# Decoder layer on one core: both row normalisations of the cross attention move from VectorE to ScalarE, and a GpSimd subtraction gets a later place

## The reference, cut to what matters

```python
def _layernorm(x, axis=-1, eps=1e-05):
    m = jnp.mean(x, axis=axis, keepdims=True)
    v = jnp.var(x, axis=axis, keepdims=True)
    return (x - m) / jnp.sqrt(v + eps)

def _L0_xattn_ref(input1, input2, theta_w, theta_b, phi_w, phi_b, g_w, g_b, ln_gamma, ln_beta, out_w, out_b):
    theta_x = jnp.einsum('ld,bdt->btl', theta_w, input2) + theta_b
    phi_x = jnp.einsum('ld,bdt->blt', phi_w, input1) + phi_b[:, None]
    p = jax.nn.softmax(jnp.einsum('btl,bls->bts', theta_x, phi_x), axis=-1)
    g_x = jnp.einsum('ld,bdt->btl', g_w, input1) + g_b
    t_x = jnp.einsum('bts,bsl->blt', p, g_x)
    mu = jnp.mean(t_x, axis=(1, 2), keepdims=True)
    var = jnp.var(t_x, axis=(1, 2), keepdims=True)
    h = jax.nn.relu((t_x - mu) * jax.lax.rsqrt(var + LN_EPS) * ln_gamma + ln_beta)
    return jnp.einsum('ol,blt->bot', out_w, h) + out_b[None, :, None] + input2

x = x + _L0_attn_ref(_layernorm(x, axis=-1), ...)
x = x + _L0_xattn_ref(_layernorm(x, axis=-1), ctx_2048, ...)
x = x + _L0_ffn_ref(_layernorm(x, axis=-1), ...)
```

## Time and profile before

| what | value |
|---|---|
| time, median of 3 runs | 3100.88 us (3097.79 to 3101.97) |
| the profiled execution's own time | 3099.93 us |
| its span, first to last instruction | 3098.2 us |
| PE busy in the span | 2804.7 us (91%) |
| DVE, ACT, POOL busy | 1327.8, 887.2, 846.1 us |
| cross attention in the span | from about 722.8 to 1134.2 us |

### The profile page before, as it was taken

How to read it: one execution, slowest core, us unless ns; L and a number is a source line. 1 busy time by engine, 2 the same in 40 slices (tenths; PEclk the granted TensorE clock), 3 DMA queues, 4 the chain that set the end, 5 groups by cost and what they waited for, 6 DMA issues and landing times.

```text
span 3098.2 us, 46522 instructions
## 1 busy us (share of the span) xinstructions
PE 2804.7 (91%) x16538; PEld 2355.9 (76%) x16538; DVE 1327.8 (43%) x2273; ACT 887.2 (29%) x1637; POOL 846.1 (27%) x1123
## 2 busy tenths in 40 slices
PE   6989999997787740799999999999999999999998
PEld 6855555476676630699999999999999999999997
DVE  6756777577888862113213213223223223223111
ACT  1126666623444422112112112112112112112110
POOL 4546777512222317201111110110210210210110
PEclk9999999998988965799999999999999999999999
DMA  3102222341212114203203213212112212122110
GB/s 103 41 2 39 46 46 46 60 112 46 81 42 80 61 39 106 66 20 105 79 25 109 73 45 95 66 58 88 60 59 85 64 65 86 55 72 82 37 48 20
DMA packets 97119, 194.60 MB, mean 63 GB/s; under 512 B 22126, under 2 KB 23822, under 8 KB 96848
## 3 DMA queue, kind: packets, MB, share of 16 engines
q1 hardware_dynamic: 75168, 131.85, 14.8%
q0 software_dynamic: 21808, 60.65, 6.3%
HBM read 148.77 MB, written 38.94 MB: 61 GB/s over the span
## 4 chain that ended last, share of the span: by engine, by line
PE 59%; issue 2%; DMA 1%; DVE 0%; POOL 0%; ACT 0%; SPq 0%; DVEq 0%; POOLq 0%
PE ex_hid L1709 29%; PE ex_acc L102 9%; PE ex_acc L103 9%; PE ex_acc L104 9%; PE ex_xb L1679 1%; DMA ex_raw<-in_w_tiles_dram 1%; DVE ex_w_l L1611 0%; ACT ex_w_h L1580 0%; DVE ex_w_l L1614 0%; DMA ex_ys<-xn_dram,ex_rows_in 0%; POOL out_dram L1561 0%; SPq L1507 0%; DMA ex_ys<-slot_table_dram 0%; ACT ex_w_h L1582 0%; DVE ex_ys L1622 0%
## 5 line engine op out<-in xcount | busy, mean ns | idle before, releaser
L1630 DVE SCALAR_TENSOR_TENSOR ex_h0l<-ex_hid,ex_h0h 128x640 fp32r<-128x640 f32 x128 | 105.6, 825 | 690.5 <-ACT ex_h0h L1589 683.2
L1630 DVE SCALAR_TENSOR_TENSOR ex_h1l<-ex_hid,ex_h1h 128x640 fp32r<-128x640 f32 x128 | 105.6, 825 | 613.8 <-ACT ex_h1h L1589 562.6
L1589 ACT ACTIVATE ex_h0h<-ex_hid 128x640 fp32r<-128x640 f32 x128 | 90.3, 706 | 739.0 <-PE ex_hid L1709 726.5
L1589 ACT ACTIVATE ex_h1h<-ex_hid 128x640 fp32r<-128x640 f32 x128 | 90.3, 706 | 737.7 <-PE ex_hid L1709 705.4
L652 DVE TENSOR_REDUCE at_nb<-at_ring 128x2 f32<-128x512 f32 (+1 forms) x384 | 246.9, 686 | 121.7 <-PE at_ring L758 121.7
L1525 POOL COPY ex_gi<-ex_slot_gather 128x1 int32 (+1 forms) x84 | 16.4, 196 | 904.9 <-PE ex_xb L1679 896.7
L102 PE MATMUL ex_acc<-ex_w_h,ex_h1h 128*128 128x512 f32 x640 | 254.8, 398 | 0.0
L102 PE MATMUL ex_acc<-ex_w_h,ex_h0h 128*128 128x512 f32 x640 | 253.4, 396 | 0.0
L103 PE MATMUL ex_acc<-ex_w_l,ex_h0h 128*128 128x512 f32 x640 | 250.3, 391 | 0.0
L103 PE MATMUL ex_acc<-ex_w_l,ex_h1h 128*128 128x512 f32 x640 | 250.2, 391 | 0.0
L104 PE MATMUL ex_acc<-ex_w_h,ex_h1l 128*128 128x512 f32 x640 | 249.8, 390 | 0.0
(11 more groups left out here) (271 smaller groups left out, 5980.0 us busy)
## 6 DMA issues: line engine op xcount, KB each, us to landing
ex_raw<-in_w_tiles_dram SPq DMA_DIRECT2D x256, 256.0 KB
x_in<-in_x_dram SPq DMA_DIRECT2D x32, 256.0 KB
act<-at_raw SPq DMA_DIRECT2D x128, 64.0 KB
at_recb<-o_rec_dram SPq DMA_DIRECT2D x16, 512.0 KB
k<-in_x_dram SPq DMA_DIRECT2D x32, 256.0 KB, 2.7
cx_ctx<-in_ctx_dram SPq DMA_DIRECT2D x16, 512.0 KB
out_dram<-cx_res SPq DMA_DIRECT2D x16, 512.0 KB
xn_dram<-cx_prob SPq DMA_DIRECT2D x16, 512.0 KB
```

The source lines that it names most:

```text
L1589: act.activation(h[f % 2][0][:], hid[:, :, 0:HB], ACT.Relu).then_inc(sm["h_hi"], 1)
L1630: dve.scalar_tensor_tensor(h[f % 2][1][:], hid[:, :, 0:HB], 0.0, f32(h[f % 2][0][:]), ALU.max, ALU.subtract).then_inc(sm["h_lo"], 1)
```

## The change

`norm_input` goes from DVE to ACT: (x - m)·r is done as r·x + (-m·r), an ACTIVATE of the Identity function with a scale and a bias per row. It stands at the head of ACT's tail, and in `front(0)` ACT does `norm_input` and `xin_hi` of each chain ahead of `ctx_hi`. The shift -m·r is made by POOL in the stage before, with two more small instructions a round. The second normalisation goes from DVE to ACT in the same form, behind `latent_hi` of theta and ahead of the splits of its own transposes; POOL makes its shift with two more small instructions a chain. And POOL's context remainder, in the tail, waits until both chains' `h_lo` are there.

```diff
@@ stage_attention, gpsimd, output projection
                 pool.tensor_tensor(t["rstd1"][:, bass.ds(CH * j, CH), 0], now, t["half"][:].to_broadcast([P, CH]),
                                    ALU.pow).then_inc(op["rstd_ready"], 1)
+                less = t["shift1"][:, bass.ds(CH * j, CH), 0]
+                pool.tensor_tensor(less, t["mv1"][:, bass.ds(CH * j, CH), 0], t["minus"][:].to_broadcast([P, CH]),
+                                   ALU.mult).then_inc(op["rstd_ready"], 1)
+                wait_apart(pool, op["rstd_ready"], 2 * j + 2, op["passed_pool"])
+                pool.tensor_tensor(less, less,
+                                   t["rstd1"][:, bass.ds(CH * j, CH), 0], ALU.mult).then_inc(op["shift_ready"], 1)
@@ stage_cross, gpsimd, tail
                 if ahead:
+                    wait_apart(pool, sm["h_lo"], CB * j + CB, sm["passed_pool"])
                     front(j + 1)
                 for c in chains:
                     n = CB * j + c
                     pool.wait_ge(sm["moments"], ONE + TPB * (n + 1))
                     pool.tensor_tensor(ve[:, c, :], mv[:, c, :, 1], t["eps"][:].to_broadcast([P, TPB]),
                                        ALU.add).then_inc(sm["eps"], 1)
+                    pool.tensor_scalar(less[:, c, :], mv[:, c, :, 0], -1.0, None, ALU.mult).then_inc(sm["rstd"], 1)
                     pool.wait_ge(sm["eps"], ONE + n + 1)
                     pool.tensor_tensor(rstd[:, c, :], ve[:, c, :], t["half"][:].to_broadcast([P, TPB]),
                                        ALU.pow).then_inc(sm["rstd"], 1)
+                    pool.wait_ge(sm["rstd"], ONE + 2 * n + 2)
+                    pool.tensor_tensor(shift[:, c, :], less[:, c, :], rstd[:, c, :], ALU.mult).then_inc(sm["shift"], 1)
@@ stage_cross, scalar
+            def norm_input(j, c):
+                n = CB * j + c
+                wait(act, sm["xin_lo"], n + 1 - CB)
+                for u in range(TPB):
+                    act.activation(xin[c][:, u, :], t["act"][:, TPB * n + u, :], ACT.Identity,
+                                   bias=t["shift1"][:, TPB * n + u, :], scale=t["rstd1"][:, TPB * n + u, :])\
+                        .then_inc(sm["xin"], 1)
             def front(j):
+                for c in chains:
+                    norm_input(j, c)
+                    xin_hi(j, c)
                 ctx_hi(j)
-                for c in chains:
-                    xin_hi(j, c)
             def tail(j, ahead):
+                if ahead:
+                    for c in chains:
+                        norm_input(j + 1, c)
...
                     latent_hi(j + 1, "theta")
                 for c in chains:
                     n = CB * j + c
+                    act.wait_ge(sm["shift"], ONE + n + 1)
+                    for u in range(TPB):
+                        act.activation(prob[c][:, u, :], res[c][:, u, :], ACT.Identity, bias=shift[:, c, u:u + 1],
+                                       scale=rstd[:, c, u:u + 1]).then_inc(sm["xn3"], 1)
+                for c in chains:
+                    n = CB * j + c
@@ stage_cross, vector
-            def norm_input(j, c):
-                n = CB * j + c
-                for u in range(TPB):
-                    dve.tensor_scalar(xin[c][:, u, :], t["act"][:, TPB * n + u, :],
-                                      t["mv1"][:, TPB * n + u, 0:1], t["rstd1"][:, TPB * n + u, :],
-                                      ALU.subtract, ALU.mult).then_inc(sm["xin"], 1)
             def front(j):
                 for c in chains:
-                    norm_input(j, c)
-                for c in chains:
                     xin_lo(j, c)
             def tail(j, ahead):
-                if ahead:
-                    for c in chains:
-                        norm_input(j + 1, c)
...
-                for c in chains:
-                    n = CB * j + c
-                    dve.wait_ge(sm["rstd"], ONE + n + 1)
-                    for u in range(TPB):
-                        dve.tensor_scalar(prob[c][:, u, :], res[c][:, u, :], mv[:, c, u, 0:1], rstd[:, c, u:u + 1],
-                                          ALU.subtract, ALU.mult).then_inc(sm["xn3"], 1)
```

More of the change, by code:

```diff
@@ L151, in _ @@
             pool.memset(t["half"][:], -0.5)
+            pool.memset(t["minus"][:], -1.0)
             pool.memset(t["eps"][:], EPS)
@@ L407, in stage_attention @@
         op = {n: s.sem("op_" + n) for n in ("wo_loaded", "wo_hi", "wo_lo", "hi", "lo", "y_ready", "x1_done", "stats",
-                                            "moments", "eps", "kept", "rstd_ready", "passed_pool", "passed_dve")}
+                                            "moments", "eps", "kept", "rstd_ready", "shift_ready", "passed_pool", "passed_dve")}
         x_loaded = [s.sem(f"op_x_loaded{c}") for c in range(CH)]
@@ L869, in stage_cross @@
         rstd = s.sb("cx_rstd", [P, CB, TPB])
+        less = s.sb("cx_less", [P, CB, TPB])
+        shift = s.sb("cx_shift", [P, CB, TPB])
         nmx = s.sb("cx_nmx", [P, CB, NTT])
@@ L886, in stage_cross @@
                  "gmv", "gsq", "gvar", "gve", "grstd", "centred", "scaled", "h_hi", "h_lo", "out", "x2", "stats",
-                 "moments", "eps", "rstd", "xn3", "x3T", "x3_hi", "x3_lo", "lgT", "lgT_kept", "logits",
+                 "moments", "eps", "rstd", "shift", "xn3", "x3T", "x3_hi", "x3_lo", "lgT", "lgT_kept", "logits",
                  "logits_kept", "passed_dve", "passed_pe", "passed_pool")
@@ L1734, in decoder_layer @@
         t["half"] = s.sb("half", [P, 1])
+        t["minus"] = s.sb("minus", [P, 1])
         t["eps"] = s.sb("eps", [P, 1])
@@ L1743, in decoder_layer @@
             t["rstd1"] = a.sb("rstd1", [P, NT, 1])
+            t["shift1"] = a.sb("shift1", [P, NT, 1])
             for n in ("theta_b", "phi_b", "g_b"):
```

## The result

| | before | after |
|---|---|---|
| median | 3097.77 us (3094.28 to 3101.97, 6 runs) | 3086.63 us (3084.44 to 3088.36, 6 runs) |
| ratio after / before | | 0.9962, 95% interval 0.9949 to 0.9975 |
| profiled execution, its span | 3099.93, 3098.2 us | 3084.44, 3082.7 us |

The change takes 11.1 us off by the medians; forecast were 3089.0 us and 11.9 off. The cross attention runs from 720.40 to the last copy of logits at 1122.31, 401.9 us, where it ran from 722.84 to 1134.05, 411.2 us. So the stage gives 9.3 of the 15.5 us by which the two spans differ. The rest isn't the change's: 2.4 lie ahead of the stage, though the change adds 0.5 there, and 3.8 behind it, where the code is the same. Such stages come out a few us apart from one execution to the next.

What follows compares the result with a forecast made beforehand. The cross attention's pass was taken as bound by a chain hopping between engines, none full. Seven passes 8.4, front 4.3, last tail -0.8 gave 11.9 us off, hence 3089.0 us; range 3079 to 3097.

Steps and rivals of the forecast that it cites:

- the likeliest case: The change works as summed, whole kernel at 3085 to 3094 us; chance 55%.
- POOL's new work: Output projection, ahead of the stage's barrier: two small POOL instructions and a wait add 0.65 us.
- The ACT normalisation: One normalisation on ACT with per-row scale and bias takes 0.81 us, each 0.71 when neighbours overlap.
- The head of the tail: `norm_input` on ACT delays the copy of `tx` by 0.62 us and PE's `phi` by 0.4 a pass.
- POOL's wait: Tail: DVE's scaled pair takes 1.4 us instead of 3.53, and the residual sum starts 1.1 us earlier.
- The second normalisation: Moved to ACT, with POOL's shift taking 1.44 us; the router starts at 886.85 instead of 888.09, 1.2 us a pass.
- clock, good: Rival: passes with a low PE clock turn to full clock, giving 3084 us; chance 6%.
- clock, bad: Rival: the four passes with good PE clock turn bad, costing 6 us, giving 3095; chance 15%.
- The front: Stage's start: ACT takes `xin` before the context, PE starts 4.3 us earlier; net 4.3, bounds 3.7 to 5.
- The last tail: With no front in it, from L962 to the router takes 6.4 us instead of 5.36; loss 0.8.
- The slower rival: POOL's moved remainder holds the residual sum L1165; each pass loses 1.7 us, 8.5 slower, 3109; chance 6%.

Runs made afterwards that it cites:

- the fourth experiment: The changed kernel with the first normalisation of the loop's tails back on DVE: 3078.22 us, ratio 0.9939 to the kernel before.
- the filled after: The changed kernel with matmuls that nothing reads in three idle gaps of PE per pass: 3070.69 us, ratio 0.9911 to the kernel before.
- the last experiment: The changed kernel with POOL's context remainder waiting for the residual sums instead of `h_lo`: 3132.02 us, ratio 1.0105 to the kernel before.
- the best version: The kernel before with POOL's wait, `xin` split before the context, and theta's remainder moved behind the router's splits, without filling matmuls: 3074.26 us, ratio 0.9928.
- the filled before: The kernel before with matmuls that nothing reads in three idle gaps of PE per pass: 3095.45 us, ratio 0.9994 to the kernel before.

## Why the prediction was right, and which step failed

**Sum.** 11.9 us off was forecast and 11.1 measured; 3086.63 lies within 3085 to 3094, the own range of the likeliest case. But the profiled stage gained 9.3, and 8.8 with the 0.5 that POOL's new work costs ahead of it, where the terms promised 11.9; and within the passes the parts differ more than the sum. That the median came so near is partly luck.

**The ACT normalisation: right.** Estimated at 0.81, one each 0.71. Measured: medians of 0.817 and 0.807 over 32 each, four in a row in 2.93 (850.64 to 853.57). The head of the tail loses 0.55 a pass (the fourth experiment), forecast was 0.4. With this move undone the median falls by 8.4, far more than the forecast gave it.

**POOL's wait: right as a mechanism, and its gain at the residual sum is the step that failed.** (1.1 us earlier in the forecast, behind the 0.4 lost at the tail's head; 1.5 counted from the centring.) The pair went to 1.41 and PE's idle 1.11 us went. But "the residual sum L1165 starts at 876.05 instead of 877.17" took PE's `phi` and `g` at full speed for granted, as in the pass that was read. "The other passes repeat it" was wrong: in before every second pass has the slow `phi`, and there the residual sum comes at 9.46, at 9.37 in the others, because the hold and the slow `phi` lie side by side. After has `phi` at the low clock in all seven passes, `g` is late, and the gain is hidden: 9.46, with the wait and without it. At full clock the step is there in full (7.87 against 9.37).

**The second normalisation: right.** From the start of POOL's `ve` to the end of the shift it took 1.32 (873.95 to 875.27), forecast 1.44. PE's transposes started 6.60 after the residual sum, forecast 6.7, and the router 10.70, forecast 10.8; before it was 10.92. Most of the 1.2 us forecast here was to come from the residual sum's being earlier; without that, 0.23 is left.

**What paid instead.** 0.85 a pass come from the router's matmuls: they are slow in no pass, where in before they are in every second. That is the rival "clock, good" in one place and "clock, bad" in another. The forecast gave both a chance, but as alternatives that moved the whole sum, and not as two halves that nearly cancel. The 0.85 has nothing to do with the reasons that the forecast gave, and that it made up for over half of the missing 1.5 is luck.

**The front: right.** PE's first `phi` matmul was forecast 4.3 us earlier, with POOL's new work ahead of the barrier counted in. Timelines of POOL, ACT, DVE and PE there, after, to be set beside the earlier trace rows:

```profile
716.08 1.01 POOL L560 TENSOR_TENSOR rstd<-op_ve,half 128x4 f32 x1 [0.24 <-POOL op_ve L557]
...
717.44 0.20 POOL L566 TENSOR_TENSOR shift<-shift,rstd  x1 [0.19 <-POOL shift L563]
...
720.40 1.52 ACT L996 ACTIVATE cx_xin<-act,shift,rstd 128x512 f32<-128x512 f32 x2 [17.54 <-PEq L97]
...
723.04 1.23 DVE L1084 TENSOR_TENSOR cx_r<-cx_xin,cx_r 128x1024 fp32r<-128x1024 f32 x1 [7.76 <-ACT cx_r L1004]
...
724.32 0.79 PE L102 MATMUL cx_bank<-cx_r,phi_w_hi 128*128 128x512 f32 x1 [11.40 <-DVE cx_r L1084]
```

PE starts 3.9 us after the first normalisation and not 8.8, so the matmul comes 4.9 sooner, counted from the stage's start. POOL's two instructions take 0.55 us from the end of `rstd` (717.09) to the end of the shift (717.64), forecast 0.65, and that comes off: 4.3, as forecast. At the first centring 4.2 of the 4.9 are left, and 3.7 after POOL's share, the low edge of the forecast's 3.7 to 5.

**The last tail: right.** From POOL's `ve` to the router 6.31 us (1111.99 to 1118.30), forecast 6.4 and 5.36 before; the loss of 0.9 was forecast as 0.8.

**The slower rival: wrong.** The residual sum beside POOL's remainder (L1184 at 869.57, POOL from 866.05 to 870.80) takes 2.72 for four, 2.71 before. Only its first 1.2 us lie under POOL. In the filled after, where it starts sooner, nearly all of it does (863.67 to 866.39), and it takes 2.72 too. POOL there:

```profile
861.41 4.75 POOL L948 TENSOR_TENSOR cx_r<-cx_ctx,cx_r 128x1024 fp32r<-128x1024 f32 x2 [3.79 <-DVE cx_r L1175]
```

The sum reads one tensor in PSUM and one in SBUF, and it isn't held. With the row statistics of the last experiment these are two forms of instruction that POOL leaves alone. Both agree with the Trainium skill's page "GPSIMD Engine Reference" (Specifications), by which POOL contends with a DVE instruction of two SBUF inputs or a two-port mode.

**Not settled.** Which gaps make the clock fall, in which pass: the idle ahead of `phi` is 2.12 us in after with a slow `phi`, and as long in a pass of before with a fast one:

```profile
865.85 0.38 PE L1268 MATMUL cx_bank<-cx_pmv,avg 128*128 128x2 f32 x2 [2.11 <-DVE cx_pmv L1127]
```

Only that filling this gap does away with the slow `phi` is shown. So it isn't shown either why the router's matmuls are fast in all passes after, and another execution may have other passes slow. And the 6 us by which the other stages of the two profiled executions differ have no cause in the diff; the medians say nothing on how much of the 11.1 is theirs.

## What to carry to other kernels

When one engine is found to hold another up, look at what else comes last at that place: the hold was worth 1.5 us a pass only where PE ran at full speed, and nothing where PE was slow. Read the granted clock stage by stage, in more than one pass, before pricing a step from one pass; where it dips behind an idle gap of some 2 us, matmuls that nothing reads can be worth more than the change (16 us here, and 9 on the best version). Do it after the waits behind which PE is late are gone: with them the median gained nothing. One profiled execution can't price what comes and goes with the clock, so take several times of each kernel and see how they spread. And first ask whether work that an engine sheds was on the path: with both normalisations left on DVE, one wait and two reorderings gave 12 us more than the change (3074.26 against 3086.63).

## What the runs showed of the hardware that was not expected

- Under POOL's run on two SBUF tensors a pair on DVE with two SBUF tensors takes 3.53 instead of 1.41 us. Row statistics (1.28 a pair) and sums with the first operand in PSUM (2.72 for four) aren't held.
- In the loop PE is never idle for longer than 2.92 us, and yet the granted clock drops to 0.5 two or three times in a pass, before and after, behind gaps of 2.1 to 2.9 us, and in the filled before behind one of 1.1. Not every such gap is followed by a drop. A drop in `phi` costs 1.5 us of a pass of 48, one in the router 1.65, and a long one instead of a short one among the transposes 1.3.
- A per-row scale and a per-row bias together make an ACT pass of 128x512 take 0.81 us, where a plain one takes 0.63.
